# Router ranks in the accumulator bank, exponential from tanh, smaller output groups, and three low halves on VectorE

## What is computed

```python
x = x + attention(layernorm_c(x))      # 7x7 windows, shifted, 12 heads of 8, relative bias and masks
t = tokens(x)
s = layernorm_t(t)
scores = s @ gate_w + gate_b           # 4 experts
probs  = softmax(scores)
masked = probs * mask_of_top_2(probs)  # on a tie the lower index wins
masked = masked / (sum(masked) + 1e-9)
h = gelu(s @ w1[e] + b1[e])            # 96 -> 384, for each of 4 experts
y = h @ w2[e] + b2[e]                  # 384 -> 96
out = t + sum over e of masked[e] * y[e]
```

## Time and profile before

| | us |
|---|---|
| median of 3 runs (lowest, highest) | 7973.55 (7973.3, 7974.85) |
| the profiled execution | 7975.47 |
| its span, first to last instruction | 7973.6 |

### The profile page before, as it was taken

One profiled execution on the slowest core, in us unless ns is written; L12 is line 12 of the kernel. 1 busy time (PEld: TensorE's weight loads), 2 busy tenths in 40 slices (PEclk: granted clock), 3 DMA queues, 4 the chain that ended last, 5 costly groups with the idle time before them and its releaser, 6 DMA issues.

```text
span 7973.6 us, 261448 instructions
## 1 busy us (share of the span) xinstructions
PE 6600.4 (83%) x98944; PEld 5272.3 (66%) x98944; DVE 6203.9 (78%) x15654; ACT 4679.9 (59%) x8959; POOL 5109.5 (64%) x3337
## 2 busy tenths in 40 slices
PE   5888888888888888888888888888888888888887
PEld 4666666666666666666666666666666666666665
DVE  6777777777777777777777778777777777777776
ACT  3566556655565556556565556555655665566554
POOL 3666666666666666666666666666666666666665
PEclk8999999999999999999999999999999999999998
DMA  1111111111111111111111111111111111111110
GB/s 48 32 30 33 31 32 30 33 31 32 29 33 31 32 29 33 32 32 29 32 32 32 30 32 32 32 30 32 32 32 30 32 32 31 32 32 32 32 29 17
DMA packets 168081, 251.65 MB, mean 32 GB/s; under 512 B 44498, under 2 KB 129106, under 8 KB 166738
## 3 DMA queue, kind: packets, MB, share of 16 engines
q1 hardware_dynamic: 166866, 234.90, 10.3%
HBM read 80.58 MB, written 38.54 MB: 15 GB/s over the span
## 4 chain that ended last, share of the span: by engine, by line
PE 38%; DVE 24%; issue 16%; POOL 16%; ACT 6%; SPq 1%; POOLq 0%; DVEq 0%; ACTq 0%; DMA 0%
POOL gexp L435 11%; PE ps_t L1027 7%; PE ps_o L1044 5%; PE ps_s L1007 5%; DVE s_max L739 4%; PE ps_s L1017 3%; PE ps_f L1111 3%; PE ps_f L1113 3%; PE ps_f L1115 3%; DVE geq L848 3%; POOL xr L457 3%; DVE ggt L851 3%; DVE geq L849 3%; DVE gden L860 2%; DVE gsel L853 2%
## 5 line engine op out<-in xcount | busy, mean ns | idle before, releaser
L447 POOL TENSOR_TENSOR g_lo<-g_sb,g_hi 128x784 f16<-128x784 f32 x1536 | 2782.2, 1837 | 998.6 <-ACT g_hi L537 998.1
L546 ACT ACTIVATE g_sb<-ps_f 128x392 f32<-128x392 f32 x3072 | 1526.8, 497 | 221.5 <-PE ps_f L957 220.2
L562 ACT ACTIVATE pt_sb<-ps_t 113x588 f32<-113x588 f32 x1024 | 674.7, 659 | 1529.5 <-PE ps_t L1027 1529.4
L457 POOL TENSOR_TENSOR xr<-y_gated,xr 112x384 f32<-112x384 f32 (+1 forms) x1024 | 905.8, 895 | 985.5 <-DVE y_gated L884 985.5
L1111 PE MATMUL ps_f<-w_hi,g_hi 128*128 128x96 f16 x9216 | 1368.9, 215 | 0.0
L1113 PE MATMUL ps_f<-w_lo,g_hi 128*128 128x96 f16 x9216 | 1367.1, 215 | 0.0
L1115 PE MATMUL ps_f<-w_hi,g_lo 128*128 128x96 f16 x9216 | 1365.0, 215 | 0.0
L557 ACT ACTIVATE p_sb<-s_sub 113x588 f32<-113x588 f32 x1024 | 714.4, 698 | 886.2 <-DVE s_sub L743 886.2
L739 DVE TENSOR_REDUCE s_max<-ps_s 113x12 f32<-113x588 f32 x1024 | 788.8, 770 | 474.5 <-PE ps_s L1017 458.3
L955 PE MATMUL ps_f<-x_hi,w_hi 128*128 128x392 f16 x3072 | 1012.6, 330 | 117.5 <-DVE x_lo L816 111.8
L1007 PE MATMUL ps_s<-bias,sel 128*64 128x392 f16 (+3 forms) x4096 | 536.5, 325 | 686.9 <-DVE s_sub L743 672.7
(11 more groups left out here) (131 smaller groups left out, 14570.4 us busy)
## 6 DMA issues: line engine op xcount, KB each, us to landing
k_st<-qk_hi SPq DMA_DIRECT2D x768, 49.0 KB, 1.9
q_st<-qk_hi SPq DMA_DIRECT2D x768, 49.0 KB, 1.9
xr<-x SPq DMA_DIRECT2D x224, 139.1 KB
out<-xr SPq DMA_DIRECT2D x224, 139.1 KB
xa<-x SPq DMA_DIRECT2D x224, 136.5 KB
k_st<-qk_lo SPq DMA_DIRECT2D x384, 49.0 KB, 2.0
q_st<-qk_lo SPq DMA_DIRECT2D x384, 49.0 KB, 1.9
xa<-x SPq DMA_DIRECT2D x224, 10.5 KB
```

The lines of the kernel that those rows point to most:

```text
L447: nc.gpsimd.tensor_tensor(g_lo[:, slot, 0:TOK], g_sb[:, chunk, :], g_hi[:, slot, 0:TOK], ALU.subtract).then_inc(lo_done, 1)
L457: nc.gpsimd.tensor_tensor(slot, y_gated[:, g % 2, 0:n * C], slot, ALU.add).then_inc(comb_done, 1)
L546: nc.scalar.activation(g_sb[:, chunk, half * STRIP:(half + 1) * STRIP], h_bank[k % 3][:, 0:STRIP], ACT.Gelu, scale=1.0 / WSCALE).then_inc( ...
```

## The change

- Groups: an expert's seven tiles are cut into 2, 2 and 3 in place of 4 and 3. There are 12 groups in a unit in place of 8, placed anew over the iterations (`GROUPS_AT`), four of them late. `y_gated` has four buffers in place of two.
- Router: GpSimd's power is gone. ScalarE takes tanh of half the difference behind its third gelu, and VectorE makes (1+t)/(1-t) of it, which is the exponential. The ranks are counted from the scores in the accumulator bank, in `router_a`, with six small comparisons. Several intermediate results of `router_b` are in bank 0.
- `router_b` stands first in VectorE's step. Then come the roundings of chunks 0 to 2 and, new on VectorE, their three low halves; then the spread keys; then the roundings of chunks 3 to 5; then the attention. GpSimd makes the low halves of chunks 3 to 11.
- ScalarE rounds one chunk in each of six iterations in place of two in one of them.
- Late work: GpSimd's last four additions wait until the second layer norm is done; VectorE's `x2_low(f, 0)` stands ahead of the last two combines; the second hidden strip waits for the combine of group 10.

```diff
-GROUP_TILES = ((0, 4), (4, 3))
-GROUPS_AT = ((0, 1), (2,), (3,), (), (), (4,), (), ())
-COMBINES_AT = ((0,), (1,), (2,), (3,), (), (), (4,), ())
-LATE_GROUPS = (5, 6, 7)
+GROUP_TILES = ((0, 2), (2, 2), (4, 3))
+PARTS = len(GROUP_TILES)
+GROUPS_AT = ((0, 1, 2), (3,), (4,), (5,), (), (6,), (7,), ())
+COMBINES_AT = ((0, 1), (2,), (3,), (4,), (5,), (), (6,), (7,))
+LATE_GROUPS = (8, 9, 10, 11)
-ROUND_AT = ((), (6, 7), (8,), (), (), (9,), (10, 11), ())
+ROUND_AT = ((), (6,), (7,), (8,), (), (9,), (10,), (11,))
-Y_BANK = (5, 7, 6, 5, 7, 7, 4, 7)
+Y_BANK = (5, 7, 6, 5, 7, 6, 7, 7, 7, 4, 7, 4)
...
             def step(f, a, b, u):
-                first_half, second_half = range(0, CPE), range(CPE, 2 * CPE)
-                for chunk in first_half:
+                for chunk in range(CPE, 2 * CPE):
                     low_part(f, chunk)
...
                 if a is not None:
                     rsqrt2(a)
-                add(f, u, 5)
-                add(f, u, 6)
-                add(f, u, 7)
-                if a is not None:
-                    gate_exp(a)
+
+                    pool.wait_ge(norm2_done, at(a, 2, 2))
+                for g in LATE_GROUPS:
+                    add(f, u, g)
...
+            def router_tanh(f):
+
+                act.wait_ge(router, at(f, N_ROUTER, 2))
+                nc.scalar.activation(gtanh[:, :, :], gsub[:, :, :], ACT.Tanh, scale=0.5 / WSCALE
+                                     ).then_inc(tanh_done, 1)
...
+                V.tensor_copy(gsc[:, :, :], sc).then_inc(router, 1)
+                dve.wait_ge(router, at(f, N_ROUTER, 3))
+
+                for e in range(EXPERTS):
+                    for f0, f1, beats in ((0, e, ALU.is_ge), (e + 1, EXPERTS, ALU.is_gt)):
+                        if f0 < f1:
+                            ins = V.tensor_tensor(ahead[:, :, e, f0:f1], sc[:, :, f0:f1],
+                                                  gsc[:, :, e:e + 1].broadcast_to([LANES, W, f1 - f0]), beats)
+                ins.then_inc(router, 1)
+                dve.wait_ge(router, at(f, N_ROUTER, 4))
+                V.tensor_reduce(rank[:, :, :], ahead[:, :, :, :], AX.X, ALU.add).then_inc(router, 1)
...
+                link(V.tensor_scalar(gden28[:, :, :], gtanh[:, :, :], -1.0, 1.0, ALU.mult, ALU.add))
+                link(V.reciprocal(gden28[:, :, :], gden28[:, :, :]))
+                link(V.tensor_scalar(powers, gden28[:, :, :], 2.0, -1.0, ALU.mult, ALU.add))
...
+            def low_part(f, chunk):
+
+                dve.wait_ge(hi_dve, at(f, N_ROUND, chunk + 1))
+                V.tensor_tensor(g_lo[:, chunk, 0:TOK], g_sb[:, chunk, :], g_hi[:, chunk, 0:TOK],
+                                ALU.subtract).then_inc(lo_dve, 1)
...
             def step(f, a, b, u):
+                router_b(f)
+                for chunk in range(CPE):
+                    round_chunk(f, chunk)
+                for chunk in range(CPE):
+                    low_part(f, chunk)
                 if a is not None:
                     spread_keys(a)
-                for chunk in range(2 * CPE):
+                for chunk in range(CPE, 2 * CPE):
                     round_chunk(f, chunk)
-                router_b(f)
```

More of the change, by code:

```diff
@@ L463, in prologue @@
                 rsqrt2((0, 0))
-                gate_exp((0, 0))
             def step(f, a, b, u):
-                first_half, second_half = range(0, CPE), range(CPE, 2 * CPE)
-                for chunk in first_half:
+                for chunk in range(CPE, 2 * CPE):
                     low_part(f, chunk)
[L470 to L473, removed]
+                for g in range(3):
+                    add(f, u, g)
                 if b is not None:
@@ L477, in step @@
                     low_part(f, chunk)
[L478 to L482, removed]
+                    add(f, u, chunk - CPE)
+                low_part(f, 9)
+                low_part(f, 10)
+                add(f, u, 6)
+                low_part(f, 11)
+                add(f, u, 7)
                 if a is not None:
                     rsqrt2(a)
-                add(f, u, 5)
-                add(f, u, 6)
-                add(f, u, 7)
-                if a is not None:
-                    gate_exp(a)
+                    pool.wait_ge(norm2_done, at(a, 2, 2))
+                for g in LATE_GROUPS:
+                    add(f, u, g)
             schedule(pool, step, prologue)
@@ L798, in residual @@
                 if before is not None:
-                    combine(before, 5)
+                    combine(before, 8)
                 sums_of(*second_part)
+                if before is not None:
+                    combine(before, 9)
                 centre(*first_part)
@@ L805, in residual @@
                 scale(*second_part)
+                x2_low(f, 0)
                 if before is not None:
-                    combine(before, 6)
-                    combine(before, 7)
-                x2_low(f, 0)
+                    combine(before, 10)
+                    combine(before, 11)
                 x2_low(f, 1)
@@ L863, in router_b @@
+                dve.wait_ge(inverse_done, at(f, 1, 1))
                 assert k[0] == N_ROUTER
@@ L904, in attention @@
                 for n in range(8):
-                    if f is not None and 0 < n < 7:
+                    if f is not None and n:
                         for g in COMBINES_AT[n]:
@@ L910, in attention @@
                     if f is not None and n == 0:
-                        combine(f, 0)
+                        for g in COMBINES_AT[0]:
+                            combine(f, g)
                     if n:
@@ L1135, in attention @@
                         experts(f, groups.pop(0))
+                        experts(f, groups.pop(0))
                     if n < 7:
@@ L1164, in attention @@
                 transpose2(a, b)
-                hidden(a, (0, 1))
+                hidden(a, (0,))
+                if f is not None:
+                    pe.wait_ge(gated, at(f, N_Y, 11))
+                hidden(a, (1,))
                 gate_scores(a)
```

104 lines of the change are left out of this document (44 added, 60 removed).

## The result

| us | before | after |
|---|---|---|
| median (lowest, highest), 4 runs each | 7973.99 (7973.3, 7974.85) | 6766.47 (6764.57, 6766.61) |
| span of the profiled execution | 7973.6 | 6762.7 |
| mean granted clock of TensorE | 0.942 | 0.996 |

After over before is 0.8485, with a 95% interval of 0.847 to 0.85: faster by 15%. The time lies in the forecast's range, but not where its likeliest case put it.

The account below looks back on a forecast made before the run. No engine is full; a chain through TensorE, VectorE and GpSimd bounds the kernel at 61.25 us a unit. Gains 1.55 + 1.2 + 1.65 - 0.1 + 1.0 = 5.3 us a unit; 7975 - 678 = 7297, so 7300 us, range 6750 to 7430.

Parts of the forecast that it names:

- The forecast's likeliest case: Whole kernel: 5.3 us gained a unit, chunk 5's rounding waiting and part of TensorE's clock regained; 7300 us, 50%.
- the rival with 28%: Last roundings on VectorE: the rounding does not wait and the clock holds; 9.3 us a unit, 6790 us, 28%.
- VectorE's work up to the first softmax: From `gmax` to the first `s_max`: router, roundings, low halves and keys sum to 13.3 us without waiting.
- The waiting rounding: Last roundings on VectorE: chunk 5's rounding waits for GpSimd's low halves, 3.1 us, making the stretch 16.4 in place of 17.95.
- the row of the power: Ordinary unit of the kernel before: GpSimd's power never delays VectorE's keys and roundings; taken as evidence for a cost of 0.
- The clock: TensorE around the first softmax: a shorter pause keeps part of its clock, gaining 1.2 us a unit, between 0 and 2.1.
- The groups: Iterations of the attention: smaller groups fit TensorE's pauses, gaining 1.65 us a unit, less 0.1 for group 7 and chunk twelve.
- The norm: Second layer norm to `gmax`: later additions and earlier `x2_low(f, 0)` gain 1.0 us a unit (0.4 to 1.3).
- The router's short instructions: `router_b` on VectorE: none over 0.3 us, as GpSimd is idle; the rival of no faster router, about 8000 us, had 2%.
- The tables: ScalarE: tanh and gelu need different tables, two more loads a unit; +165 us, 7465 us, 5%.
- One wait, 6980: Last roundings on VectorE: the rounding waits for one low half, 1.6 us, and the clock holds; 7.8 us a unit, 12%.

Follow-up runs that it names:

- experiment 5: Kernel after, with a 0.26 us one-input sum and a wait for its end between VectorE's keys and last three roundings: 7102.65 us.
- experiment 1: Kernel after, with four extra reductions of the scores, results unused, ahead of the first `s_max`: 7321.53 us.
- experiment 11: Kernel after, with the old groups of 4 and 3 tiles and their old iterations and combines: 6958.61 us.
- 8: Kernel after, with `router_b` behind the last roundings, its intermediate results in the accumulator bank: 7185.66 us.
- 9: Kernel after, with `router_b` behind the last roundings, its intermediate results in SBUF: 7534.55 us.
- experiment 10: Kernel after, with the bank's slices replaced by three small SBUF tiles, `router_b` left first: 6769.34 us.
- 3: Kernel after, with all twelve low halves on GpSimd and the keys directly behind the first three roundings: 7046.64 us.
- experiment 7: Kernel after, with the twelve keys ahead of VectorE's three low halves instead of behind them: 6767.48 us.
- 12: Kernel after, with keys ahead of VectorE's low halves, first softmax ahead of the roundings of chunks 3 and 4, chunk 5's behind the second softmax: 6878.62 us.
- 4: Kernel after, with the rounding of chunk 3 ahead of the twelve keys instead of behind them: 7100.95 us.
- 6: Kernel after, with the rounding of chunk 3 behind eight of the twelve keys: 7097.06 us.
- experiment 2: Kernel after, with two extra reductions of the scores ahead of the first `s_max`: 7097.69 us.

## Why the prediction was right and where it was wrong

The forecast's likeliest case did not come. Its range held because it had been stretched down to the rival with 28%, and that rival came.

- **VectorE's work up to the first softmax: right.** 13.3 us were worked out and 13.25 measured. `router_a` took 1.63 (1.6), `router_b` 2.10 (1.9), three roundings 1.44 (1.45), three low halves 2.65 (2.85), the keys 4.00 (4.05), and the last three roundings 1.43 (1.45). A low half takes 0.97 us by itself, against the estimate of 1.0 from the earlier trace rows. They are 0.89 apart. TensorE has the hidden strips done by then, as forecast, but it waits 0.89 us in the mean for the keys before the first scores, which the forecast did not have.
- **The waiting rounding: the step that failed.** I added 3.1 us from the earlier trace rows, "the row of the same two instructions in the same order", and it costs 0. The same two instructions were not the same situation: experiment 5 changes only what stands before them and has 1.5 us of waiting at that place. The earlier trace rows differed in two things. The roundings ahead of that one had been held themselves (4.42 us the one before it), and GpSimd's low halves came one directly behind the other; which of the two decided is not shown. I gave the row of the power 28% and the other 50% because of the likeness of the instructions. But the earlier trace rows is one unit of 128, and the forecast had not weighed how the same two instructions met in the other 127 of the kernel before. GpSimd's low half there, in the unit of the earlier trace rows:

```profile
4113.59 3.45 POOL L447 TENSOR_TENSOR g_lo<-g_sb,g_hi 128x784 f16<-128x784 f32 x1
```

  It is recorded as started behind the third of six roundings (in 31 units behind the second). The others started after it, and none waited. The record of the power lasts until 4115.56, so this row does not show alone which of the two the low half waited for, but it spoke for the rival.
- **The clock: its sign was right, its size was not.** I took 1.2 us between 0 and 2.1. Without the delay the two distances shrank by 7.38 - 5.39 = 1.99, near the upper end. With 2.75 us of delay (experiment 1) they shrank by only 0.41, near the lower end. So 1.2 fits neither case.
- **The groups: right.** 1.65 less 0.1 were forecast, the two units show 1.54, and experiment 11 has 1.51 a unit. The iterations are 3.29, 3.05, 3.31, 3.04 and 3.37, against 3.2, 3.04, 3.32, 3.04 and 3.35.
- **The norm: right.** 1.0 was forecast and 9.67 - 8.71 = 0.96 measured. The second `scale` takes 0.46 us in every unit, where the earlier trace rows had 0.97. Its parts were not taken apart by a run.
- **The router's short instructions: right.** None is over 0.33 us (the first reciprocal, 0.329 at most). That it is the early place that does it, and not the bank, experiments 8 to 10 show.
- **The tables: the rival did not come.** ScalarE after, tanh and the loads of tables (times, total us, mean ns):

```profile
L539 ACT ACTIVATE gtanh<-gsub x128: 217/218/218, 113.8 to 6715.4; 112x28 f32<-112x28 f32 x128
```
```profile
L520 ACT ACT_TABLE_LOAD x255 | 327.2, 1283 | 4.5
```

  The kernel before had two groups of loads too, x255 and x1, with the same 327.2 us. 128 tanh between gelus brought none. The Trainium skill (ScalarE: Activation LUTs, "Table sets: the hidden batching unit") lists tanh with exp and not with gelu. That a tanh between gelus would need a load of its own is not borne out here.
- **The rival "no wait", 6790.** It is the case that came, with 9.3 us a unit against 9.2 in the two units and 9.5 over the spans. "One wait, 6980" priced 1.6 us with the clock kept. Its terms sum to 5.3 + 1.5 + 0.9 = 7.7 us and not 7.8, which is 12 us. Experiment 5 is close to that case, with 0.3 us for the break besides, at 7103: the wait is right, but the clock does not survive it.

What stays open is what decides who goes next. GpSimd lost one turn where VectorE's row was long and the low half was asked for between two roundings: in the kernel after, in 3 (the last roundings), 7, 8 and 9. It won the turn where the row was short or had been held: in the earlier trace rows, 3 (the first roundings) and 5. In 12 there was no row: the low half was already running when the rounding was issued. It also won in 4 and 6, between two keys behind a long row. One rule for all of them would have to say more than that the row is long. That VectorE already has its next instruction in line when GpSimd asks fits most of them, but the trace does not record when an instruction is put in line, so this is argued and not shown. Three more parts of the change were not undone by themselves: tanh in place of the power, ScalarE's new places for its roundings, and the new order behind the second layer norm.

## What to carry to other kernels

The wait of one engine for another can't be priced from a row of the same two instructions alone: look at what stood before them on the engine that would be held, count in how many repetitions each row stands, and where two rows disagree, keep a price for each. Put short dependent instructions where the other engine has no work; here it then made no difference in which memory their operands lay (experiment 10). Before an order starts one consumer earlier, ask which later result it delays, and whether cover is left for that one. And when an experiment meets a forecast number, compare the stretches too: two errors can cancel in the sum.

## What the runs showed of the hardware

**Asking first is not always going first.** In the kernel after a low half of GpSimd issued at 4023.97 waits 0.74 us (2.42 against 1.68), while VectorE's rounding that is issued some 0.3 us later takes 0.56. The Trainium skill (SBUF — State Buffer, "Who interferes with whom") says that whoever issues first gets the shared pair of ports for the whole instruction. Where a VectorE instruction waited in experiments 3, 4, 5, 6 and 12, the low half had been issued first, which agrees. In the kernel after, in 7, 8, 9 and at the last roundings of 3 the low half was issued first too and did not get its turn; there the measurement decides.

**TensorE's clock and short pauses.** The waits of TensorE for VectorE ahead of the first or the second scores, over the span (total us, times, longest): two lines of the kernel after, then one of experiment 7 and one of the kernel with two extra reductions.

```profile
PE ps_s L1018 <- DVE k_bd L728: 112.9, 127, 1.2
PE ps_s L1018 <- DVE s_sub L738: 65.0, 129, 1.7
```
```profile
PE ps_s L1018 <- DVE s_sub L738: 137.0, 129, 1.7
```
```profile
PE ps_s L1024 <- DVE s_sub L744: 254.5, 129, 3.2
```

The mean of each pause, and in how many of the 127 units the granted clock fell to 0.50:

| kernel | mean pause, us | units with the clock at 0.50 | mean clock |
|---|---|---|---|
| after | 0.89 (keys), then 0.50 | 0 | 0.996 |
| experiment 7 | 1.06 | 1 | 0.996 |
| 12 | 1.42 (low half) | 58 | 0.982 |
| 2, two reductions | 0.84 (keys), then 1.97 | 97 | 0.973 |
| 5 | 0.81 (keys), then 2.34 | 81 | 0.976 |
| 3 | 2.47 (keys) | 111 | 0.970 |
| 4 and 6 | 2.78 (keys) | 127 | 0.966 |
| 8 | 3.07 | 127 | 0.960 |
| 1, four reductions | 0.81 (keys), then 3.32 | 115 | 0.958 |
| 9 | 5.40 | 127 | 0.939 |

In the main a longer pause goes with more units at 0.50, but not in step: experiment 5 has the longer pause and fewer such units than 2, and 1 has fewer than 4. So the length of the one pause does not settle it alone. Where it began, 1.5 us of extra VectorE work cost 2.6 (experiment 2).
